# Three-layer conditional transformer on one core: TensorE's score matmuls of two ticks placed together, one transpose for the row maxima, and no square root or gate exponential on ScalarE

## What is computed

```python
qkv = (xn @ w_qkv + b_qkv).reshape(B, N, 3, H, hd)
q, k, v = (qkv[:, :, 0], qkv[:, :, 1], qkv[:, :, 2])
q = _ln(q, 1e-05, qn_g, qn_b)
k = _ln(k, 1e-05, kn_g, kn_b)
attn = jnp.einsum('bqhd,bkhd->bhqk', q, k) * scale
attn = jax.nn.softmax(attn, axis=-1)
o = jnp.einsum('bhqk,bkhd->bqhd', attn, v).reshape(B, N, C)
...
topk_logits, topk_idx = jax.lax.top_k(gate_logits, TOP_K)
gates = jax.nn.softmax(topk_logits, axis=-1)
```

## Time and profile before

| | before |
|---|---|
| median of 3 runs | 2012.87 us (2006.87 to 2023.93) |
| the profiled execution, its own time | 2018.31 us |
| its span | 2016.5 us |
| PE busy | 1834.8 us, 91% |
| DVE busy | 1197.3 us, 59% |
| ACT busy | 959.6 us, 48% |
| POOL busy | 587.7 us, 29% |
| ACT table loads | 29 (L1530 9, L1460 8, L1519 7, L1470 4, L1312 1) |
| attention stages, about | 276 to 540, 736 to 1037, 1204 to 1484 us |

### The profile page before, as it was taken

How to read it: one execution, slowest core, us unless ns; L and a number is a source line. 1 busy time by engine, 2 the same in 40 slices (tenths; PEclk the granted TensorE clock), 3 DMA queues, 4 the chain that set the end, 5 groups by cost and what they waited for, 6 DMA issues and landing times.

```text
span 2016.5 us, 28869 instructions
## 1 busy us (share of the span) xinstructions
PE 1834.8 (91%) x10144; PEld 1225.2 (61%) x10144; DVE 1197.3 (59%) x2585; ACT 959.6 (48%) x1744; POOL 587.7 (29%) x597
## 2 busy tenths in 40 slices
PE   7998689998898798998889989999898799999998
PEld 6775444443487663444348764444357688898997
DVE  5775267777364566776735567777534555555554
ACT  2332247666745347786664426776553422222221
POOL 3553112222555332433344413222331311101000
PEclk9999579999999888999999989999889999999999
DMA  5100133333100213232310203333201000001000
GB/s 193 67 2 2 47 101 106 95 90 99 37 11 1 76 58 95 66 95 78 87 42 4 82 3 117 106 90 93 82 1 45 27 24 19 30 14 34 1 24 24
DMA packets 69598, 114.29 MB, mean 57 GB/s; under 512 B 15091, under 2 KB 30115, under 8 KB 69167
## 3 DMA queue, kind: packets, MB, share of 16 engines
q1 hardware_dynamic: 69456, 112.45, 18.2%
HBM read 81.19 MB, written 30.73 MB: 56 GB/s over the span
## 4 chain that ended last, share of the span: by engine, by line
PE 72%; ACT 10%; DVE 8%; issue 4%; DMA 3%; SPq 2%; POOL 2%; ACTq 0%; DVEq 0%; POOLq 0%
PE ps L1685 24%; PE ps L1769 14%; PE ps L1738 7%; PE ps L1724 7%; PE ps L1834 5%; PE ps L1706 4%; ACT Pr L1519 3%; DMA heads_t<-stage 2%; PE ps L1809 2%; PE ps L1568 2%; DVE negmax L1083 2%; PE ps L1557 1%; ACT xn L1411 1%; ACT HQ L1494 1%; DVE X L1101 1%
## 5 line engine op out<-in xcount | busy, mean ns | idle before, releaser
L1083 DVE TENSOR_REDUCE negmax<-ps 128x1 f32<-128x512 f32 x768 | 489.3, 681 | 248.3 <-PE ps L1706 244.2
L1519 ACT ACTIVATE Pr<-ps 128x512 f32<-128x512 f32 x768 | 410.3, 603 | 193.1 <-PE ps L1724 191.9
L1530 ACT ACTIVATE g<-ps,b1col 128x512 f32<-128x512 f32 x216 | 148.3, 687 | 455.8 <-PE ps L1685 435.0
L1272 DVE CAST G<-g 128x512 fp32r<-128x512 f32 x216 | 121.9, 564 | 308.1 <-ACT g L1530 307.3
L1769 PE MATMUL ps<-W2a,G 128*128 128x288 f32 x1728 | 267.6, 306 | 7.2 <-DVE G L1274 5.8
L1724 PE MATMUL ps<-QK 55*128 55x512 f32 x768 | 236.7, 510 | 40.0 <-ACT Pr L1519 29.9
L1769 PEld LDWEIGHTS ps<-W2a,G 128*128 128x128 f32 x1728 | 249.6, 195 | 20.7 <-DVE G L1274 10.5
L1706 PE MATMUL ps<-QK 54*128 54x512 f32 x768 | 196.6, 442 | 28.1 <-DMA QK<-heads_t 11.1
L1738 PE MATMUL ps<-Pr,V 128*32 128x512 f32 x1536 | 218.1, 641 | 0.0
L1724 PEld LDWEIGHTS ps<-QK 55*128 55x128 f32 x768 | 91.1, 190 | 207.5 <-ACT Pr L1519 111.9
L1274 DVE TENSOR_TENSOR G<-g,G 128x512 fp32r<-128x512 f32 x216 | 167.0, 773 | 7.4
(11 more groups left out here) (212 smaller groups left out, 2516.9 us busy)
## 6 DMA issues: line engine op xcount, KB each, us to landing
QK<-heads_t SPq DMA_DIRECT2D x192, 144.0 KB
heads_t<-stage SPq DMA_DIRECT2D x96, 252.0 KB
QK<-heads_t SPq DMA_DIRECT2D x192, 72.0 KB
raw<-in_w SPq DMA_DIRECT2D x18, 432.0 KB
raw<-in_w SPq DMA_DIRECT2D x12, 576.0 KB
WA<-in_ada_w SPq DMA_DIRECT2D x3, 1728.0 KB
heads_t<-stage SPq DMA_DIRECT2D x24, 144.0 KB
QK<-W1a SPq DMA_DIRECT2D x192, 2.0 KB, 2.6
```

Of the source, the lines that this page charges most:

```text
L1083: dve.tensor_reduce(negmax[:, m % 2, t, h:h + 1], ps[:, row_bank(l, s, i), :], AX, ALU.max, negate=True).then_inc(a_free, 1)
L1272: dve.tensor_copy(G[:, n % 3, 0, :], g32[:, n % 2, :]).then_inc(g_hi, 1)
L1519: act.activation(Pr[:, t % 2, 2 * half + pair, :], ps[:, (16 * s + u) % 3, :], ACT.Exp, scale=SCALE).then_inc(b_free, 1)
L1530: act.activation(g32[:, n % 2, :], ps[:, 4, :], ACT.Gelu if l == 1 else ACT.Gelu_apprx_tanh, bias=b1col[:, e, s % FT:s % FT + 1]).then_inc ...
```

## The change

Three things are changed.

1. **PE's order.** At an even attention tick PE now does the scores of that tick and of the next one (keys, queries, keys, queries), then the values, then the even tick's tiles, then the odd tick's tiles. The orders of all other engines stay as they are. The banks stay as they are.
2. **Row maxima.** `negmax` is laid out by head and tile, so that one transpose gives 16 rows of 128. ACT copies 16x128; each of the four DMAs reads four partitions of `mrow`.
3. **No square root and no small exponential on ACT.** The inverse root is made on DVE from a first guess on the bits of the number and three Newton steps, one in `root` and two in `inverse`. The gate's exponential is a power with base e on POOL, from a tile `euler` that is filled once.

The core of the diff:

```diff
 LAG = {
...
-    "ACT": dict(ym=0, scale=0, root=1, ln1=0, ln2=0, qk=0, tok=0, max=0, split=0, bias=0, wg=0, gexp=0),
+    "ACT": dict(ym=0, scale=0, ln1=0, ln2=0, qk=0, tok=0, max=0, split=0, bias=0, wg=0),
...
-    "POOL": dict(mean1=1, mean2=1, ln1=1, ln2=1, qk=1, out=1, proj=1, tok=1, root=3, split=1, centre=1, fin=1, wg=1,
+    "POOL": dict(gexp=0, mean1=1, mean2=1, ln1=1, ln2=1, qk=1, out=1, proj=1, tok=1, root=3, split=1, centre=1, fin=1, wg=1,
...
-        mrow = W1[0][96:100, 4, 0:2 * N].rearrange("p (z n) -> p z n", z=2)
+        mrow = W1[0][96:112, 4, 0:256].rearrange("p (z n) -> p z n", z=2)
...
-                    sp.dma_start(QK[row:row + 1, s % 4, 0, i % 2, :].bitcast(F32),
-                                 mrow[i:i + 1, m % 2, :].bitcast(F32)).then_inc(mrow_in[m % 2], 16)
+                    sp.dma_start(QK[row:row + 1, s % 4, 0, i % 2, :].bitcast(F32).rearrange("o (t n) -> o t n", t=TT),
+                                 mrow[TT * i:TT * i + TT, m % 2, :].bitcast(F32)).then_inc(mrow_in[m % 2], 16)
...
+                elif kind == "gexp":
+
+                    pool.wait_ge(logits, i + 1)
+                    pool.tensor_tensor(tmp4[:, 1, :, :], euler[:, :, :], tmp4[:, 0, :, :], ALU.pow).then_inc(cw_exp, 1)
+                    pool.wait_ge(cw_exp, i + 1)
...
+            def newton(r, t, v):
+
+                dve.tensor_tensor(t, r, r, ALU.mult).then_inc(dve_done, 1)
+                dve.wait_ge(dve_done, step())
+                dve.scalar_tensor_tensor(out=t, in0=t, scalar=-0.5, in1=v, op0=ALU.mult, op1=ALU.mult).then_inc(dve_done, 1)
+                dve.wait_ge(dve_done, step())
+                return dve.scalar_tensor_tensor(out=r, in0=t, scalar=1.5, in1=r, op0=ALU.add, op1=ALU.mult)
...
-                    v = qvar[:, ROOT[key] % 2, :, :]
-                    dve.tensor_scalar(v, v, 1.0 / HD, QK_EPS, ALU.mult, ALU.add).then_inc(var_set, 1)
...
+                    dve.tensor_scalar(v, v, 1.0 / HD, QK_EPS, ALU.mult, ALU.add).then_inc(dve_done, 1)
+                    dve.wait_ge(dve_done, step())
+                    dve.tensor_scalar(r.bitcast(I32), v.bitcast(I32), -0.5, ROOT_SEED, ALU.mult, ALU.add).then_inc(dve_done, 1)
+                    dve.wait_ge(dve_done, step())
+                    newton(r, t, v).then_inc(dve_done, 1)
...
-                if kind == "root":
-                    act.wait_ge(var_set, ROOT[key] + 1)
-                    act.activation(qroot[:, 1, :, :], qvar[:, ROOT[key] % 2, :, :], ACT.Sqrt).then_inc(root_set, 1)
-                    return
...
-                if kind == "gexp":
-                    act.wait_ge(logits, i + 1)
-                    act.activation(tmp4[:, 1, :, :], tmp4[:, 0, :, :], ACT.Exp).then_inc(cw_exp, 1)
-                    return
...
-                    act.activation(mrow[:, m % 2, :], bank[0:4], ACT.Copy).then_inc(misc_free, 1)
+                    act.activation(mrow[:, m % 2, :], bank[0:16, 0:128], ACT.Copy).then_inc(misc_free, 1)
...
-                    for t in range(TT):
-                        ins = pe.transpose(bank[0:4, 128 * t:128 * t + 128], negmax[:, (STEPS * l + i) % 2, t, :], ident[:, :])
+                    ins = pe.transpose(bank[0:16, 0:128], negmax[:, (STEPS * l + i) % 2, :, :].rearrange("p h t -> p (h t)"), ident[:, :])
...
+                if what == "a" and u % 2 == 0:
+                    for later in range(2):
+                        for i in (2 * (u + later), 2 * (u + later) + 1):
+                            key_scores(l, s, i)
+                        if s + 2 < STEPS:
+                            for i in (2 * (u + later), 2 * (u + later) + 1):
+                                query_scores(l, s + 2, i)
                 if what == "a":
-                    for i in (2 * u, 2 * u + 1):
-                        key_scores(l, s, i)
-                    if s + 2 < STEPS:
-                        for i in (2 * u, 2 * u + 1):
-                            query_scores(l, s + 2, i)
                     if u == 0 and s > 0:
                         values(l, s - 1, TT - 1)
```

More of the change, by code:

```diff
@@ L1 @@
 from contextlib import ExitStack
+import math
 import numpy as np
@@ L8 @@
 F32R = mybir.dt.float32r
+I32 = mybir.dt.int32
 ALU = mybir.AluOpType
@@ L39 @@
 CONSTS = 25
+ROOT_SEED = float(0x5F3759DF)
 SKP = 2048
@@ L380, in build @@
         neghalf = rest("neghalf", [128, H])
+        euler = rest("euler", [128, TT, 4])
         xn = rest("xn", [128, TT, C + 64])
@@ L394, in build @@
         qkcol = rest("qkcol", [126, QT, 2])
-        negmax = rest("negmax", [128, 2, TT, 4])
+        negmax = rest("negmax", [128, 2, 4, TT])
         rsum = rest("rsum", [128, 16])
@@ L540, in build @@
         tok_var = sem("tok_var")
-        var_set = sem("var_set")
-        root_set = sem("root_set")
         inv_set = sem("inv_set")
@@ L948, in work @@
                     low_weights(i)
+                elif kind == "gexp":
+                    pool.wait_ge(logits, i + 1)
+                    pool.tensor_tensor(tmp4[:, 1, :, :], euler[:, :, :], tmp4[:, 0, :, :], ALU.pow).then_inc(cw_exp, 1)
+                    pool.wait_ge(cw_exp, i + 1)
                 elif kind == "wg":
+                    pool.memset(euler[:, :, :], math.e).then_inc(pool_done, 1)
+                    pool.wait_ge(pool_done, pool_step())
                     pool.wait_ge(wg_hi, 3)
@@ L1082, in negmax_unit @@
                 h = 2 * half + pair
-                dve.tensor_reduce(negmax[:, m % 2, t, h:h + 1], ps[:, row_bank(l, s, i), :],
+                dve.tensor_reduce(negmax[:, m % 2, h, t:t + 1], ps[:, row_bank(l, s, i), :],
                                   AX, ALU.max, negate=True).then_inc(a_free, 1)
@@ L1230, in work @@
                 elif kind == "root":
-                    dve.wait_ge(tok_var, TT * (ROOT[key] + 1))
-                    v = qvar[:, ROOT[key] % 2, :, :]
-                    dve.tensor_scalar(v, v, 1.0 / HD, QK_EPS, ALU.mult, ALU.add).then_inc(var_set, 1)
+                    n = ROOT[key]
+                    r, t, v = qroot[:, 0, :, :], qroot[:, 1, :, :], qvar[:, n % 2, :, :]
+                    dve.wait_ge(tok_var, TT * (n + 1))
+                    if n > 0:
+                        dve.wait_ge(qn_ready, TT * n)
+                    dve.tensor_scalar(v, v, 1.0 / HD, QK_EPS, ALU.mult, ALU.add).then_inc(dve_done, 1)
[3 more added lines that the diff above has]
+                    newton(r, t, v).then_inc(dve_done, 1)
+                    dve.wait_ge(dve_done, step())
                 elif kind == "centre":
@@ L1244, in work @@
                     r, t, v = qroot[:, 0, :, :], qroot[:, 1, :, :], qvar[:, n % 2, :, :]
-                    dve.wait_ge(root_set, n + 1)
-                    if n > 0:
-                        dve.wait_ge(qn_ready, TT * n)
-                    dve.reciprocal(r, t).then_inc(dve_done, 1)
+                    newton(r, t, v).then_inc(dve_done, 1)
                     dve.wait_ge(dve_done, step())
-                    dve.tensor_tensor(t, r, r, ALU.mult).then_inc(dve_done, 1)
-                    dve.wait_ge(dve_done, step())
-                    dve.scalar_tensor_tensor(out=t, in0=t, scalar=-0.5, in1=v, op0=ALU.mult, op1=ALU.mult).then_inc(dve_done, 1)
-                    dve.wait_ge(dve_done, step())
-                    dve.scalar_tensor_tensor(out=r, in0=t, scalar=1.5, in1=r, op0=ALU.add, op1=ALU.mult).then_inc(inv_set, 1)
+                    newton(r, t, v).then_inc(inv_set, 1)
                 elif kind == "warm":
```

## The result

The changed kernel took 2231.4 us (median of 4 runs, 2225.1 to 2232.7) against 2015.7 us (median of 4) for the kernel before: a ratio of 1.105, with a 95% interval of 1.101 to 1.109. The forecast was slower, at 2140 us with a range of 2035 to 2215. The sign was right; the size was 91 us short and outside the range. The profiled execution of the changed kernel took 2225.07 us, against 2018.31 for that of the kernel before: +206.8, and this is the sum to be explained.

The account below looks back on a forecast made before the run. TensorE (PE), busy 98.6 of 100 us in the third layer's attention, was taken as the bound. 2018.3 + 113 (order) - 18 (tables) + 30 (clock) = 2143; less 5.4 for the median 2138, stated as 2140 us, range 2035 to 2215.

Parts of the forecast that it names:

- What bounds the kernel: In the third layer's attention PE is busy 98.6 of 100 us, so only TensorE's own order or waits move the time.
- SS: Two ticks' score matmuls (each S: two key, two query) in a row on PE: 1.95 us, 2.56 behind a qk tile's eviction.
- What joining gives: Even and odd ticks' tile matmuls run as one on PE: 0.38 us less per qk pair, -0.4 per proj pair.
- The rival that the blocks are free: Two ticks' scores in a row on PE take only 1.34 us, so the kernel gets faster, 1954 us; chance 0.05.
- The other pairs: Attention tick pairs other than qk, each worked out alike; with the qk pairs the order costs 113 us.
- The clock, +30: New long PE waits at some 30 places; half lose 2 us each to half clock: +30 us, bounds 0 and 60.
- the clock goes with it: Rival: every second pair with a second tile drops PE's clock, 140 us in place of 30, about 2250; chance 0.12.
- Tables, -18: Fewer ACT table loads: 14 us saved at three roots meeting max, 4 at other roots, none at the gate.
- hidden by its idle 29%: The root's added small operations, 11 us more on DVE, cost nothing because DVE has idle time; unhidden, 11 us.
- The gate's power: The gate's exponential as a power on POOL takes 1.1 to 4.5 us; taken as zero cost, 18 us at worst.
- only max: Ten attention pairs whose only tile work is the row maximum: -0.33 us each, -3 us together.
- The signs: Profile after: slower paired scores, some 60 us more key waits, attention stages 30 to 50 us longer each, more low-clock slices.

## Why the prediction was right or wrong

**What bounds the kernel.** Right. PE, and the order alone made the whole change (2228 us with nothing but the order).

**SS costs 1.95, and 2.56 behind an eviction.** Right: 2.02 behind a proj tile (457.64 to 459.66) and 2.47 behind a qk tile (446.73 to 449.20). The waits of PE at the keys for ACT's Pr grew from 29.9 to 96.2 us, by 66, where some 60 was said.

```profile
PE ps L1736 <- ACT Pr L1531: 96.2, 167, 1.9
```

**What joining gives.** The qk tile took 1.81 in one piece (444.92 to 446.73) against 1.73 worked out, and proj 2.14 (455.50 to 457.64). Before, proj's parts stood at 1300.36 to 1301.52 and 1302.19 to 1303.36, together 2.33. A join is worth 0.2 us and not the 0.4 that I took for proj, which over 36 pairs is 7 us.

**The rival that the blocks are free.** Refuted. The Trainium skill's rule on changing the tiling mode (TensorEngine Tiling (Array Packing), Key Properties) would have let fewer changes be a gain; the row that bears on it is the 0.18 us of a joined qk pair, and the two score groups, with the fourth key's wait in them, show no gain.

**The other pairs, sum 113.** Too high as a sum. The max and v pair took 4.72 (worked out: 4.70), so that piece was sized well, yet with the lost clock taken off, the three stages grew by only 64 (29, 6, 30; root and tables are in this). With the order alone they grew by 106, or some 90 (an estimate) less the 16 of the shorter maximum that the 113 has in it. The step that failed is the adding: in layer 1 I charged the long waits and the clock as if both would be paid. At half clock ACT and DVE kept their speed (an exponential of 0.60 us, a maximum of 0.68) and the banks were free when PE came: 4.59 us for a pair with no wait at all. A wait that vanishes there is paid for in clock.

**The clock, +30 with bounds of 0 and 60.** This is the term that was mis-sized: 137 us by the windows (101 with the order alone). Its 107 us too few would by themselves move 2140 to 2247, outside the range. From 2143 to the profiled 2225 it is +107 for the clock, -31 for order and tables together (95 forecast, 64 found) and +6 outside the stages. Two choices made it. I let half of 30 places lose 2 us each, from one window of 4 us that I had cut myself just behind a stall, without asking when the clock came back (it did about 850, 2 us beyond that window). Measured over a stage, slow stretches lasted 7 us before and 12 after (18 in layer 1). The kernel before showed its own: layer 1 at a mean clock of 0.92 over 299 us is 24 us lost for three root stalls and a few others, where my price gave 6. And I had the rival ("the clock goes with it", 2250), and gave it 0.12 on the argument that waits of 0.9 us are too short to matter. One such wait doesn't; one in every pair, with a second gap at bank 7, does, as the added matmuls show: filled, they give 93 of layer 1's 126 us back. That the rival's number came so near the measured 2231 is in part luck: it has 70 slow stretches of 4 us where 18 more and longer ones came, and it keeps the 113 that was too high.

**Tables, -18.** Wrong by sign within the kernel: root and gate together cost 22 us (2035.9 against 2014.0). The stalls of the earlier trace rows did go. The step that failed is "hidden by its idle 29%": a mean of a whole window says nothing about the moment. The chain stood ahead of the query maxima, and its end released POOL's QN and then a transfer that PE needed. In the changed kernel as a whole, PE was late enough itself to hide the transfers (waits for them in all: 13.9 us, before 11.1). The 18 us of gain are missing there too: 2231.4 with everything, 2228.3 with the order alone. Beside the clock this is a small part of the miss.

**The gate's power.** 3.06 us against the bounds 1.1 to 4.5, cost zero: right.

**The maximum.** Worth 15 us alone, as 48 x 0.33 says; the sum's -3 for "only max" was for ten of them, and the others' share was inside the pairs. In the joined order the saving does not show in the total.

**The range.** Its upper end was added up short. The terms that I named for it, 30 for the clock, 29 for the unhidden work and 28 for a quarter of the 113, make 2227 and not 2200. 2231 is outside that too.

**The signs.** The waits before the keys and the two S came as described. Layers 0 and 2 grew by 49 and 44 us, inside the 30 to 50; layer 1 grew by 108, though PE's idle time (length less busy, in the windows above) grew by 26 us there and by 28 and 29 in the others, and that is the last sign named: where the waits do not show it, it is the clock.

## What to carry to other kernels

Before putting two groups of one kind side by side on TensorE, count the banks of the group against its reader's pace, and keep other work between them: here the values between the two score groups were worth 178 us, while the exponential took 602 ns in either order. Where a change opens a gap in every repetition, price the clock from the mean granted clock of a whole stage that already has such gaps, not from the stretch behind one stall, and carry the slow level and the waits as alternatives and not as a sum. A chain moved to an engine with idle time is hidden only if its end isn't what a transfer waits for: look for who is released last, and move the chain's end before moving its work.

## What the runs showed of the hardware that I had not expected

- **A busy TensorE stayed at its lower level.** From 854.38 on, in layer 1 of the changed kernel, matmuls run without a wait through 855 to 865 us, and the windows above show 5.00 of 5.00 us busy at 0.50. Before that, from 850 to 855, it was busy 3.38 of 5.
- **Useless matmuls paid for themselves.** 221 of them (442 records) took 54 us or more of PE's time, and the stage became 41 us shorter.
- **Small VectorE operations are sometimes five times as long.** In the kernel with the root alone, one operation of the root on a 128x64 tile took 1.23 us while POOL was at work, and 0.23 when it was not:

```profile
767.23 1.23 DVE L1089 SCALAR_TENSOR_TENSOR qroot<-qroot,qvar 128x64 f32<-128x64 f32 x1
...
772.61 0.23 DVE L1089 SCALAR_TENSOR_TENSOR qroot<-qroot,qvar 128x64 f32<-128x64 f32 x1
```

```profile
767.10 1.28 POOL L914 TENSOR_TENSOR stage<-act,stage 126x512 fp32r<-126x512 f32 x1 [4.33 <-ACT stage L1519]
...
774.02 2.93 POOL L940 TENSOR_TENSOR QN<-QN,qroot 128x288 f32<-128x288 f32 x4 [5.64 <-DVE qroot L1091]
```

The DVE operation begins inside POOL's first row and ends at 768.46, just after it (768.38). Of the 72 operations of the Newton steps in this kernel, the 63 with no POOL instruction beside them took at most 0.23 us; of the nine that overlapped one, five took 0.69 to 2.68. The maxima on DVE, which read PSUM, keep their 0.68 us. That the two engines share something is my reading; no run isolated it.
